# Channel attention: the scans read the keys from PSUM, and the own queries' sums move one step

## The reference

```python
Q = (x @ Wq + bq).reshape(b, s, H, C) * inv_sqrt_c        # H = 16, C = 64
K = (x @ Wk + bk).reshape(b, s, H, C)
V = (x @ Wv + bv).reshape(b, s, H, C)
scores = jnp.einsum('bshq,bshk->bshqk', Q, K)             # a product of two scalars
mask = jnp.triu(jnp.ones((C, C), dtype=bool), 1)
w = jax.nn.softmax(jnp.where(mask, -inf, scores), axis=-1)
attn = jnp.einsum('bshqk,bshk->bshq', w, V).reshape(b, s, HID)
return attn @ Wo + bo
```

## Time and profile before

| | |
|---|---|
| median of 3 runs | 3225.54 us (3220.49 to 3230.01) |
| the profiled execution, its own time | 3221.55 us |
| its span | 3217.7 us |
| TensorE's granted clock, mean | 0.946 |
| DVE busy | 2244.1 us (70%) |
| PE busy | 2606.6 us (81%) |
| ACT busy | 1852.5 us (58%) |
| POOL busy | 1556.9 us (48%) |

### The profile page before, as it was taken

The page is one execution under the profiler, slowest core; times in us unless marked ns, Lnnn a source line. Parts: engine busy times, 40 slices in busy tenths (PEclk is TensorE's granted clock), DMA queues, the critical chain, the costliest instruction groups (busy, mean ns, idle before and its releaser), DMA issues. The chain is left out here.

```text
span 3217.7 us, 52070 instructions
## 1 busy us (share of the span) xinstructions
PE 2606.6 (81%) x19172; PEld 2068.6 (64%) x19172; DVE 2244.1 (70%) x4214; ACT 1852.5 (58%) x4363; POOL 1556.9 (48%) x1473
## 2 busy tenths in 40 slices
PE   1998799889987998777688876888768887688867
PEld 0465556555655565577577766777667776677757
DVE  2167516751675168523999969999699996999964
ACT  0364536453645355422877748777487774877743
POOL 0141314131413142312987729877298772987725
PEclk8999999989998999888999998999989999899988
DMA  9400000000000000075000000000000000000005
GB/s 239 130 2 1 5 10 2 1 5 10 2 1 5 10 2 1 18 274 185 4 8 1 1 4 4 7 1 1 4 4 7 1 1 4 4 7 1 1 28 161
DMA packets 75363, 93.12 MB, mean 29 GB/s; under 512 B 9325, under 2 KB 61340, under 8 KB 74985
## 3 DMA queue, kind: packets, MB, share of 16 engines
q1 hardware_dynamic: 24388, 51.54, 4.9%
q10 hardware_dynamic: 45540, 27.93, 3.6%
q0 software_dynamic: 5184, 10.29, 1.0%
HBM read 61.58 MB, written 28.62 MB: 28 GB/s over the span
## 5 line engine op out<-in xcount | busy, mean ns | idle before, releaser
L1701 POOL TENSOR_TENSOR arena<-arena 128x1536 f32<-128x1536 f32 (+9 forms) x480 | 1035.7, 2185 | 293.1 <-DVE arena L1765 247.7
L1569 PE MATMUL psum<-ident,arena 128*128 128x128 f32 (+7 forms) x7168 | 880.6, 282 | 293.3 <-ACT arena L1670 286.2
L1569 PEld LDWEIGHTS psum<-ident,arena 128*128 128x128 f32 (+7 forms) x7168 | 806.9, 139 | 397.5 <-ACT arena L1670 351.1
L1660 ACT ACTIVATE arena<-arena 128x64 f32<-128x64 f32 (+7 forms) x2048 | 708.2, 485 | 122.0 <-PE psum L1578 122.0
L1765 DVE TENSOR_TENSOR arena<-arena,psum 128x1536 f32<-128x1536 f32 (+9 forms) x480 | 494.7, 1064 | 52.8 <-ACT arena L1670 45.1
L1670 ACT ACTIVATE arena<-arena 128x1536 f32<-128x1536 f32 (+2 forms) x288 | 406.7, 1416 | 177.5 <-DVE arena L1751 177.5
L901 POOL TENSOR_SCALAR arena<-arena 128x512 f32<-128x512 f32 (+3 forms) x512 | 263.9, 532 | 498.5 <-DVE arena L864 498.3
L1751 DVE TENSOR_TENSOR arena<-arena,psum 128x1536 f32<-128x1536 f32 (+9 forms) x480 | 493.8, 1063 | 14.3 <-POOL arena L1701 12.5
L822 ACT ACTIVATE arena<-arena 128x512 f32<-128x512 f32 (+3 forms) x512 | 281.8, 552 | 183.2 <-DVE arena L857 183.2
L518 POOL TENSOR_SCALAR veps<-mv 128x1 f32<-128x1 f32 x112 | 21.5, 192 | 615.2 <-DVE mv L513 610.5
L775 PEld LDWEIGHTS psum<-ident,arena 128*128 128x128 f32 x1280 | 142.4, 145 | 169.9 <-ACT arena L833 84.7
(11 more groups left out here) (274 smaller groups left out, 3619.2 us busy)
## 6 DMA issues: line engine op xcount, KB each, us to landing
arena<-in_L_ffn_W SPq DMA_DIRECT2D x39, 768.0 KB
arena<-in_L_ffn_W SPq DMA_DIRECT2D x23, 514.0 KB
rows_d<-xrow ACTq DMA_DIRECT2D x1, 9504.0 KB, 51.0
y_d<-xrow ACTq DMA_DIRECT2D x1, 9216.0 KB
arena<-rows_d SPq DMA_DIRECT2D x62, 66.0 KB
y_d<-arena POOLq DMA_DIRECT2D x39, 64.0 KB
arena<-in_L_ffn_h_w ACTq DMA_DIRECT2D x2, 1024.0 KB
wa<-in_L_attn_W_attn ACTq DMA_DIRECT2D x1, 1536.0 KB
```

The lines of the kernel that those rows point to most:

```text
L1569: last = nc.tensor.matmul(ps[ch.half][0:rows, to:to + P], buf[:, c:c + rows], ident[:], start=first, stop=False, is_transpose=True, skip_g ...
L1660: nc.scalar.activation(by_key[:, 0:HD - r, j], keys[:, h, 0:HD - r], ACT.Exp, bias=NB[:, j:j + 1], scale=Q3[tt % 2][:, j:j + 1]).then_inc( ...
L1701: last = nc.gpsimd.tensor_tensor(of_piece(D3[n % 5], piece), q, keys_on(K3[tt % 2], k, nk, w), ALU.mult)
```

## The change

Banks 5 and 6 of PSUM hold the two accumulators of half 1 (numerators and denominators), which stand idle from `finish` in step 8 until the next tile begins. For this, the two banks of `psD` change places. Under the name `psK` the two banks together take the keys in the order "head, channel". ACT writes them with the same copy as `KH`, behind it, two more copies of 512 columns for each tile. `KH` stays, because the own exponentials read it. From tile 1 on ACT waits, ahead of the copy, for `finish` of half 1. The scans read `psK` in place of `KH`. PE waits for the scans ahead of the first sum of a tile.

The own queries' exponentials are spread over steps 2 to 13 in place of 1 to 14, and what PE and DVE do with them moves one step ahead. The first denominators are summed in step 14 and the last numerators in step 17, and nothing of it is left for step 0 of the next tile.

```diff
-        psD = [psum[:, 6, :], psum[:, 7, :]]
+        psD = [psum[:, 7, :], psum[:, 6, :]]
+        psK = psum[:, 5:7, :].rearrange("p a n -> p (a n)")
...
-        OWN_STEPS = range(1, NC - 3)
+        OWN_STEPS = range(2, NC - 4)
...
-        OWN_DEN = {NC - 3: (0, 1), NC - 2: (2, 3)}
-        OWN_W = {NC - 2: (0, 1), NC - 1: (2, 3)}
-        OWN_NUM = {NC - 1: (0, 1), 0: (2, 3)}
+        OWN_DEN = {NC - 4: (0, 1), NC - 3: (2, 3)}
+        OWN_W = {NC - 3: (0, 1), NC - 2: (2, 3)}
+        OWN_NUM = {NC - 2: (0, 1), NC - 1: (2, 3)}
...
-            return psum[:, (4, 5, 3, 2)[j], :] if tt == 0 else scratch
+            return psum[:, (4, 7, 3, 2)[j], :] if tt == 0 else scratch
...
-            idle_work(6, 24)
+            idle_work(4, 24)
...
+                    if c == 0:
+                        pe.wait_ge(s["scan"], tt + 1)
...
-                if n >= NC - 1:
-                    of = tt if c == NC - 1 else tt - 1
-                    for o in OWN_NUM.get(c, ()):
-                        pe.wait_ge(s["own_w"], of * PARTS + o + 1)
-                        sum_own(psA, o).then_inc(s["own_num"], 1)
                 if n == NALL:
                     break
+                for o in OWN_NUM.get(c, ()):
+                    pe.wait_ge(s["own_w"], tt * PARTS + o + 1)
+                    sum_own(psA, o).then_inc(s["own_num"], 1)
...
                 if j < 2:
-                    by_head = KH[tt % 2].rearrange("p (h c) -> p c h", h=NH)[:, j * HD // 2:(j + 1) * HD // 2, :]
-                    nc.scalar.activation(by_head, qk_bank(tt, j).rearrange("p (c h) -> p c h", h=NH), ACT.Copy, scale=HD ** -0.5)\
-                        .then_inc(s["kh"], 1)
+                    if tt > 0:
+                        act.wait_ge(s["attn"], 2 * tt - 1)
+                    for to in (KH[tt % 2], psK):
+                        by_head = to.rearrange("p (h c) -> p c h", h=NH)[:, j * HD // 2:(j + 1) * HD // 2, :]
+                        last = nc.scalar.activation(by_head, qk_bank(tt, j).rearrange("p (c h) -> p c h", h=NH), ACT.Copy,
+                                                    scale=HD ** -0.5)
+                    last.then_inc(s["kh"], 1)
...
-                    last = nc.vector.tensor_tensor_scan(dst, f[:], KH[tt % 2], 0.0, ALU.add, op)
-                then(last)
+                    last = nc.vector.tensor_tensor_scan(dst, f[:], psK, 0.0, ALU.add, op)
+                last.then_inc(s["scan"], 1)
+                dve.wait_ge(s["scan"], tt + 1)
```

More of the change, by code:

```diff
@@ L485, in transformer @@
             "d", "e", "w", "den", "num", "attn", "proj", "qk", "qk_sb", "v", "kh", "prod", "chain", "rows",
-            "own", "own_den", "own_w", "own_num", "q_ps", "neg")}
+            "own", "own_den", "own_w", "own_num", "q_ps", "scan", "neg")}
         def x_ready(eng, stage):
```

## The result

The changed kernel takes 3235.23 us (median of 20 runs, 3228.62 to 3237.54), the kernel before, run beside it, 3225.64 (3219.56 to 3232.10). The ratio is 1.0026, 95% interval 1.0018 to 1.0034. I forecast 3215, inside 3205 to 3233. So the change costs 9.6 us where I expected a gain of 11, and the median lies 2 us outside the range.

The account below looks back on a forecast made before the run. DVE was taken to set the pace. Per batch, -0.32 (tile 0), -0.82, -1.32 and -0.2 (tiles 1 to 3) made -2.7 us, four times -10.7: 3214.9 against the median, stated as 3215, range 3205 to 3233.

Parts of the forecast that it names:

- Part 1: DVE's scans reading keys from PSUM: pairs of 4.48 us, no longer excluding POOL's products, 7.92 us of DVE saved per batch.
- Part 3: Own queries in steps 2 to 13: 1.65 us more ahead of step 11's exponential, chain starting 1.82 sooner in tile 1.
- The wait in step 11: DVE's wait for ACT ahead of the scans: to grow from 1.7 to 2.2 us to about 3.0 to 3.6.
- signs named for a wrong forecast: Pairs over 5 us, weigh(0) waiting over 3 us for PE, or DVE waiting for ACT in steps 12 to 14, tiles 0 to 2.
- the rate of a plain copy: Price p of each new ACT copy into PSUM, taken as 0.48 us from a range of 0.48 to 0.87.
- stride or no stride: ACT's copies into PSUM: strided price 0.87 us as in SBUF (chance 0.22, 3227 us) or dearer (0.09, 3238).
- the only strided ACT write of the trace: Argument for the rival at p = 0.87: ACT's strided copy into SBUF; that rival's chance 0.22.
- It fits with a few tenths to spare: Fill of the next tile's values, 3.9 us early before, still in time behind PE's second own sum of 3.5 us.
- A miss under 3 us would come off the wait in step 11: If the fill came late by under 3 us, DVE's wait for ACT in step 11 would absorb it.
- The end of tile 3: PE's last product at 1901.2 instead of 1901.66: 2.7 us for step 14's matmuls plus 23.4 of work, about -0.2.
- DVE sets the pace: Bound of a steady tile: DVE busy 88.3 of 91.3 us, the other engines 70 to 76.
- 8 x p: Eight new ACT copies per batch on the path, two each at the start and in three tiles, p = 0.48 us each.

Follow-up runs that it names:

- e3: Changed kernel with the copy into psK written without a stride, so the scans read keys in another order; 3238.04 us, 1.0022 of the kernel before.
- e6: Changed kernel with own work in its old steps, keys moved only into psK, KH copied from there in step 16; 3197.57 us, 0.9898 of before.
- e10: Changed kernel with the fill of the next tile's values ahead of the own sums in step 17; 3230.68 us, 0.9997 of the kernel before.
- e11: Kernel before with one scan in place of two, the running minimum left out; 3210.89 us, 0.9935 of the kernel before.
- e2: Changed kernel with own work back in its old steps; scans from PSUM and both copies stay; 3228.21 us, 0.9994 of the kernel before.
- e5: Changed kernel with scans reading KH in SBUF again, the copies into PSUM kept but unused; 3262.65 us, 1.0092 of the kernel before.
- e1: Kernel before with only the own work's move; scans read KH, no new copies; 3241.80 us, 1.0033 of the kernel before.
- e4: Changed kernel with eight small filler matmuls for PE at the end of each of steps 6 to 13; 3279.38 us, 1.0158 of the kernel before.
- e8: Kernel before, unedited, profiled once more; 3228.99 us, where the first trace had 3221.55.
- e9: Changed kernel with twelve filler matmuls behind the sum of step 13 in every tile; 3250.56 us, 1.0066 of the kernel before.

## Why the prediction was wrong

**Right.** Part 1: pairs at 4.46 us, the scans and POOL's products no longer in turn (those beside the pair of tile 0 take 3.59 us, as alone). Part 3 in its counting. From the start of the own exponentials to the exponential of step 11 in tile 0 there were 44.64 us; with five exponentials more (1.65), two copies (1.24), one step's exponential less (1.37) the count gives 46.16. Measured are 1592.98 - 1545.92 = 47.06, and most of the missing 0.90 is ACT's one stop for PE in step 9 (0.80), in batch 1 alone. The wait in step 11 came out at 3.43 to 3.53. Of the signs named for a wrong forecast one showed, once: DVE waits 0.75 us for ACT in step 13 of tile 2 of batch 2.

**The copy was mis-sized, by 0.14 us.** I took the rate of a plain copy. Two per tile make 0.28 us, three tiles 0.84, and the start 0.09: 0.93 us per batch. By the forecast's own sum that leaves -1.8 of -2.7. The choice that I thought decisive, stride or no stride, isn't one: e3 has the same 0.63 us without. e6 shows 0.52 for the same write behind another instruction. (The copy into `KH` wasn't "the only strided ACT write of the trace" either: the own exponentials write with a stride of 128 values. No term hung on that.) The Trainium skill's rule on short lines in PSUM ("Advanced Engine Details and Errata", "Memory Cachelines") speaks of matmuls; for ACT's writes no run here shows a cost of it. What it says elsewhere, that ACT writes PSUM faster than SBUF ("ScalarE: Activation LUTs", "Step-by-step: what each stage is for"), agrees for the strided write, 0.52 to 0.62 against 0.87, and not for the plain one, 0.63 (e3) against 0.48, though these two stand behind different instructions.

**The step that failed: the cover of the V fill, and PE's clock behind it.** Twice the forecast leaned on durations of PE from the trace of before, and both times they no longer held.
- *"It fits with a few tenths to spare"*: the fill had 3.9 us of room, and an own sum of 3.5 was put ahead of it, which left 0.4. But the sum of step 14 takes 1.5 to 1.7 us longer at the lower clock, and PE has no gap behind it to make that up. In the whole stage weigh(0) waits ten times, once in tile 1 of each batch for 0.25 us and six times in tiles 2 and 3 for 0.7 to 1.7; in the kernel before never.
- *"A miss under 3 us would come off the wait in step 11"*: wrong as well. The wait delays the next subtractions, and these ACT's exponentials, which stand in a chain without a gap: the 0.38 and 0.55 us of the lines above, 0.93 together. In batches 2 and 4 the fourth pair of scans starts 1.0 us later than in e10, where the fill stands first and nothing waits for it. A wait of DVE for ACT doesn't take up a delay that ACT's chain gets as well.
- *The end of tile 3.* I took 2.7 us for the 24 matmuls of step 14 and 23.4 for the rest. PE is unbroken from there, so where that group runs at the lower clock (batch 1, and all four of e10), up to 4.51 - 2.84 = 1.67 us come on top. In batches 2 to 4 of the changed kernel the slow group is that of step 13; there the gap behind it takes up most, and 0.46 us remain.

With these the sum for a batch closes to within a few tenths. Forecast -2.7; the copies +0.93 and the clock in tile 3 +1.67 give -0.1; e10, which has both and no wait for the fill, measures +0.2. Of the 0.3 between, 0.23 are a stop of ACT for PE's own sums ahead of the first own exponential of tile 2. The changed kernel itself stands at +0.65 and +0.75 in batches 2 and 4 (the fill's 1.0 more, 1.2 less for where the slow group falls, and waits for the fill in tile 3), at -0.4 in batch 3, which waits for no fill in tile 2, and at +2.6 in batch 1, whose start and step 9 fell on a lower clock too, +0.5 and +0.9. The mean is +0.9.

**A premise that failed: "DVE sets the pace".** It was busy for 88 of 91 us, and I read that as the bound. Take the distance between two pairs of scans with the own work as before. With a scan less and ACT's work unchanged (e11) it is 90.5. e2 has 2 x 0.62 us of ACT more than that ahead of step 11, and comes to 91.8. e6 has 2 x (0.87 - 0.52) = 0.7 less, and comes to 89.85. So each tenth of ACT's work there is a tenth of the tile. Of the 4.3 us that e11 takes out of the second pair, 1.0 arrive in the tile, and of the 2.6 to 3.2 out of the third, 0.8. The forecast did book most of DVE's gain as a longer wait, so its sum didn't rest on the premise alone; but it hid how the gain could be had. The rule "ACT's copies are on the path" was in it with 8 x p, and its reverse, that taking two away pays in full, was not. With the own work moved it is otherwise: there the first own exponential no longer waits for PE, and DVE's work behind step 11 is on the path too. Between the second pair and the third e5 takes 92.7 us and the changed kernel 90.6, so the 2.1 us of the pair arrive in full.

**The own work's move was worth nothing.** By the forecast's own terms it costs 1.65 + 0.31 = 1.96 us in tile 0 without the gain at the start (e1 measures 2.0), and brings 1.82 in tiles 1 and 2 each against 1.65 more work. Against e2, which has the same copies and scans, e10 shows its full account: +1.96 in tile 0, -1.2 and -0.7 to -1.3 in the next two, about nothing in the last, together -0.3 to +0.2. With it come 10 or 11 exponentials a step in place of 9, longer gaps of PE (2.1 us for 1.5) and the lower clock in 26 to 36 groups (3 with the fillers of e4), where before had 19 and 14 and the versions with part 1 alone 5 (e2) and 4 (e6). Alone it loses 11 us (e1), on top of e6 5.6. e1 has no wait of weigh(0) for the fill (but one of 0.12 us): its longer scans hold DVE back by 2.1 us. So it is the two parts together that uncover the fill.

**What stays open.** The stage of the profiled execution is 3.6 us longer than before (4 x 0.9), while the medians differ by 9.6. The profiled execution was among the fastest of 20 and had the highest clock of them, and e8 shows 7 us of difference outside the stage for one and the same kernel. What a slower execution looks like can be seen in e3, whose instructions take as long as those of the changed kernel: weigh(0) waits in all twelve tiles that have a fill ahead of them, for 0.2 to 1.7 us, three batches end at 384.7 to 384.9, and the stage is 10 us longer than before. That fits the medians, in which e10, the fill put first, takes nearly all of the loss back; that the other 19 executions were like e3's is not shown. And why the clock falls in steps 13 and 14 is half open. The count goes with the own work's move and with PE's idle time over the steps (29 without, 3 with the fillers of e4), but not with the one gap ahead alone, which I held for the cause (e9). Why the kernel before has 14 to 19 slow sums and e2, with the own work in the same steps, 5, no run shows.

## What to carry to other kernels

An engine that is busy for 97% of a tile needn't set its length: take a piece of its work away (here one scan, an edit of two lines) and see how much of it comes back, and do so again when the lists of the other engines have changed, before pricing a change by it. Where work leans on "a few tenths to spare" behind a long unbroken run of TensorE, price the run at the lower of the two clocks as well, and follow the delay through every engine in the loop, since a wait further on absorbs it only if that wait's own chain isn't delayed with it. And a copy that only a later reader needs belongs where its engine is idle: kept late, the keys' second copy turned a loss of 0.3% into a gain of 1.0%.

## What was not expected of the hardware

- A copy of 512 fp32 columns by ACT from PSUM to PSUM, start to start: 0.62 us behind a copy with a stride of 64 values into SBUF, with or without a stride of its own (e3: 0.63), and 0.52 with its stride behind a plain copy (e6). A plain copy PSUM to SBUF takes 0.48, the strided one 0.87.
- One copy of 1024 columns PSUM to SBUF takes 0.90 us, less than two strided ones of 512 by 0.84.
- The granted clock fell to its lower level for the first group of PE's unbroken run though PE had been busy for 4.82 of 5 us, with a gap of 1.1 behind them (e4); with those fillers this happened 3 times in the stage, without them 29 times.
- In a pair of scans with one operand in PSUM, DVE shows nothing of POOL's products beside it: 32 scans within 2259 to 2287 ns, before 2283 to 4396.
- Where a scan with two SBUF inputs and POOL's products exclude each other, they don't always take turns: in e11 one scan is held for 4.5 of its 6.77 us while POOL runs through the rest of a product and three more.
